# Routing half of the tokens of the first expert phase inside the recurrence, and the other half beside the expert tiles

## What is computed

```
logits = h @ router_w.T                      # 2048 x 8 experts
probs = softmax(logits)
vals, idx = top_k(probs, 2)
vals = vals / vals.sum(axis=-1)
# for each expert: y = (silu(gate) * up) @ dp.T, weighted by its vals and summed
```

## Time and profile before

| | us |
|---|---|
| median of 3 runs | 1005.97 |
| lowest and highest | 1000.86, 1021.48 |
| the profiled execution, its time | 1002.44 |
| the profiled execution, its span | 1000.6 |
| PE, DVE, ACT, POOL busy | 714.5, 504.5, 290.2, 286.6 |

### The profile page before, as it was taken

One profiled execution on the slowest core, in us unless ns is written; L12 is line 12 of the kernel. 1 busy time (PEld: TensorE's weight loads), 2 busy tenths in 40 slices (PEclk: granted clock), 3 DMA queues, 4 the chain that ended last, 5 costly groups with the idle time before them and its releaser, 6 DMA issues. The chain is left out here.

```text
span 1000.6 us, 13964 instructions
## 1 busy us (share of the span) xinstructions
PE 714.5 (71%) x4667; PEld 551.6 (55%) x4667; DVE 504.5 (50%) x1074; ACT 290.2 (29%) x561; POOL 286.6 (29%) x360
## 2 busy tenths in 40 slices
PE   2078898964524999971246999999999750999980
PEld 1056676743522776650135777787777550677660
DVE  5828697796270223545535455645564244222433
ACT  1014323231001444430102334433444300444430
POOL 2300111201037103417610233423343407402305
PEclk9997798885655999995555778977987955999995
DMA  9700000000123334422155442244220033434534
GB/s 318 253 1 0 1 1 1 1 0 0 43 85 127 121 101 141 130 76 81 37 65 64 65 65 34 41 57 65 33 34 2 1 80 120 143 101 122 174 122 126
DMA packets 63225, 75.78 MB, mean 76 GB/s; under 512 B 9410, under 2 KB 57930, under 8 KB 62550
## 3 DMA queue, kind: packets, MB, share of 16 engines
q1 hardware_dynamic: 57014, 58.11, 24.4%
q0 software_dynamic: 6144, 16.79, 5.3%
HBM read 33.56 MB, written 28.57 MB: 62 GB/s over the span
## 5 line engine op out<-in xcount | busy, mean ns | idle before, releaser
L974 PE MATMUL bank<-f_wgu,f_xt 128*128 x368 | 131.5, 481 | 6.5 <-ACT f_xt L1032 3.3
L1136 DVE TENSOR_TENSOR f_hid<-f_act_g,bank 128x176 f32<-128x176 f32 x92 | 31.1, 338 | 177.9 <-ACT f_act_g L1039 177.9
L911 POOL DMA_INDIRECT f_back<-ys,f_slots x64 | 63.0, 984 | 171.6 <-DMA ys<-f_yout 140.2
L997 PE MATMUL bank<-f_wd,f_hT 88*128 x368 | 95.2, 381 | 0.0
L974 PEld LDWEIGHTS bank<-f_wgu,f_xt 128*128 128x128 f32 x368 | 67.2, 195 | 40.9 <-issue 16.3
L900 POOL DMA_INDIRECT xs<-xn,f_slots x64 | 62.9, 983 | 68.3 <-DVE f_lv L1122 27.4
L1431 POOL TENSOR_SCALAR_AFFINE_SELECT b_prob<-b_prob 128x512 f32<-128x512 f32 x60 | 38.2, 637 | 150.7 <-ACT b_prob L1721 150.7
L1721 ACT ACTIVATE b_prob<-bank 128x1024 f32<-128x1024 f32 x60 | 61.5, 1025 | 58.6 <-PE bank L1553 58.3
L997 PEld LDWEIGHTS bank<-f_wd,f_hT 88*128 88x128 f32 x368 | 62.9, 190 | 5.7
L959 PE MATMUL bank<-ident_sb,f_xin 128*128 128x128 f32 x184 | 37.2, 286 | 38.9 <-DMA f_xin<-xs 38.4
L1795 DVE COPY_PREDICATED bank<-b_later,bank 128x512 f32<-128x512 int32 x60 | 41.4, 690 | 38.8 <-PE bank L1524 36.9
(11 more groups left out here) (294 smaller groups left out, 1659.4 us busy)
## 6 DMA issues: line engine op xcount, KB each, us to landing
f_xin<-xs SPq DMA_DIRECT2D x92, 128.0 KB, 2.2
ys<-f_yout SPq DMA_DIRECT2D x92, 128.0 KB, 1.7
xs<-f_zero SPq DMA_DIRECT2D x2, 2944.0 KB, 21.6
b_QS<-b_qh SPq DMA_DIRECT2D x32, 128.0 KB, 4.4
b_KS<-b_kh SPq DMA_DIRECT2D x32, 128.0 KB, 4.9
f_wd<-in_wd SPq DMA_DIRECT2D x4, 968.0 KB
f_wgu<-in_wgu SPq DMA_DIRECT2D x2, 1408.0 KB, 8.6
x_tok<-in_x SPq DMA_DIRECT2D x4, 512.0 KB, 5.6
```

The source lines that it names most:

```text
L911: pool.indirect_dma_start(back[:, n % GB, e], None, ys[h], bass.IndirectOffsetOnAxis(slots[:, h, e, i:i + 1], 0)).then_inc(got[n % GB], 16)
L974: mm = pe.matmul(psG[:, g % 2, 0:2 * FH], xt[:, g % 2, k * P:(k + 1) * P], w["gu"][:, k, bass.ds(e, 2 * FH)], start=k == 0, stop=k == KD - 1)
L997: mm = pe.matmul(psY[:, g % 2, 0:D], hT[:, g % 2, k * P:(k + 1) * P], wd[:, k, bass.ds(e, D)], start=k == 0, stop=k == 1)
```

## The change

The expert phase's state and semaphores move into one object, `Routed`, that lives through the whole program (`m` in the diff), and the routing chain is cut into named pieces of the class `Routing`.

- In the first phase, half 0 is routed in the recurrence. Iteration 2 has its logits (32 matmuls after `value_or_gate(3, 3)`) and its pieces `take`, `compare_equal`, `compare`, `choose`, `take_counts` on DVE; iteration 3 has `experts`, `slots`, `difference` behind `mean_squares`. PE waits for `TAKEN` ahead of `project_out` and for `COPIED` ahead of `betas`, since the PSUM banks are shared. POOL issues 12 of the 16 scatters between the last chunk's `rms` and its `tail_pool`, and 4 behind it.
- In the first phase itself only the logits of half 1 stand ahead of the tiles. The rest of its routing is spread over steps 1 to 9, its scatters come when `slots` is done in step 5, its exponential in step 8.
- In the second phase (`HOIST[1]` is False) half 0 is routed ahead of the tiles as before, and half 1 beside them. `ranks` of half 0 now stands ahead of the logits of half 1.
- The ranks are copied from PSUM to SBUF, one more operation per half. In the first phase SP issues the `wd` DMAs behind the loads of tiles 0 and 1. Logits and ranks go to another PSUM bank. The norm of the combined tokens is written to `xn`.
- The same pieces run in the same order within a half, except that `both` is made ahead of `pick`. `at` is None and `SPREAD_COMBINE` False, so code under them does nothing here.

```diff
+        ROUTED_AT = NCH // 2
+        SENT_AHEAD = 12
...
+                    if it == ROUTED_AT:
+                        pe.wait_ge(tl.xl_ready, now(it - 1))
+                        pe_logits(pe, m, xTh, xTl, 0, psY[:, 0])
                     rms_spread(it)
...
                         value_or_gate(it + 1, VT + 1)
+                    if it == ROUTED_AT:
+                        pe.wait_ge(m.route, routed(0, 0, TAKEN))
                     project_out(it)
+                    if it == ROUTED_AT:
+                        pe_ranks(pe, m, 0, 0, psB[:, 0])
+                        pe.wait_ge(m.route, routed(0, 0, COPIED))
                     if ahead:
                         betas(it + 1)
...
+                pairs = [(i, c) for i in range(NTH) for c in range(2)]
                 for it in range(0, NCH):
                     pool.wait_ge(ms_ready, now(it))
                     pool.wait_ge(rT_ready, before(it))
                     pool.tensor_tensor(rms[:], ms[:], minus_half[:, 0:TPC * HA], ALU.pow).then_inc(rms_ready, 1)
+                    if it == NCH - 1:
+                        for i, c in pairs[:SENT_AHEAD]:
+                            pool_scatter(pool, m, xn, 0, 0, i, c)
                     tail_pool(pool, tl, it)
+                for i, c in pairs[SENT_AHEAD:]:
+                    pool_scatter(pool, m, xn, 0, 0, i, c)
...
+                first = Routing(dve, m, 0, 0)
                 for it in range(NCH):
                     ahead = it + 1 < NCH
                     if ahead:
                         start(it + 1)
                     mean_squares(it)
+                    if it == ROUTED_AT + 1:
+                        first.experts()
+                        first.slots()
+                        first.difference()
                     if ahead:
                         decays(it + 1)
                         taps(it + 1, 0)
                     rms_split(it)
                     if ahead:
                         taps(it + 1, 1)
+                    if it == ROUTED_AT:
+                        first.take(psY[:, 0])
                     outputs(it)
+                    if it == ROUTED_AT:
+                        first.compare_equal()
+                        first.compare()
+                        first.choose()
                     if ahead:
                         taps(it + 1, 2)
+                    if it == ROUTED_AT:
+                        first.take_counts(psB[:, 0])
+                    if ahead:
                         taps(it + 1, 3)
                     tail_stats_dve(dve, tl, it, add=True)
...
+RANKS_AT, SHARES_AT = 3, 8
...
+TAKEN, RANKED, COPIED, EXPERTS_KNOWN, SLOTS_KNOWN, DIFF_KNOWN, SHARED = 2, 10, 12, 19, 29, 32, 35
...
+def pe_ranks(pe, m, turn, h, dst):
+    pe.wait_ge(m.route, routed(turn, h, RANKED))
+    chosen = m.both[:].rearrange("p e i -> p (e i)")
+    pe.matmul(dst[:, 0:NE * NTH], m.tri[:], chosen, start=True, stop=True)
+    pe.matmul(dst[:, NE * NTH:2 * NE * NTH], m.ones[:], chosen, start=True, stop=True).then_inc(m.pre_ready, 1)
...
+    def choose(self):
+        dve, m = self.dve, self.m
+        by_expert = m.rank[:].rearrange("p t e -> p e t")
+        self.step(dve.tensor_reduce(m.rank[:], m.cmp1[:].rearrange("p t (e j) -> p t e j", e=NE), AX.X, ALU.add))
+        self.step(dve.tensor_scalar(m.both[:], by_expert, 1.5, None, ALU.is_lt))
+        self.step(dve.tensor_scalar(m.pick[:, 0], by_expert, 0.0, None, ALU.is_equal))
+        self.step(dve.tensor_scalar(m.pick[:, 1], by_expert, 1.0, None, ALU.is_equal))
+        assert self.n == RANKED
+
+    def take_counts(self, src):
+        dve, m = self.dve, self.m
+        dve.wait_ge(m.pre_ready, 2 * self.turn + self.h + 1)
+        self.step(dve.tensor_copy(m.pre[:], src[:, 0:NE * NTH]))
+        self.step(dve.tensor_copy(m.tot[:], src[:, NE * NTH:2 * NE * NTH]))
...
+    def shares(self):
+        dve, m, h = self.dve, self.m, self.h
+        mine = slice(h * NTH, (h + 1) * NTH)
+        self.n = DIFF_KNOWN
+        dve.wait_ge(m.ex_done, 2 * self.turn + h + 1)
+        self.step(dve.tensor_scalar(m.den[:], m.ratio[:, h], 1.0, None, ALU.add))
+        self.step(dve.reciprocal(m.share[:, 0, mine], m.den[:]))
+        self.step(dve.tensor_tensor(m.share[:, 1, mine], m.share[:, 0, mine], m.ratio[:, h], ALU.mult))
+        assert self.n == SHARED
+
+
+def act_ratio(act, m, turn, h):
+    act.wait_ge(m.route, routed(turn, h, DIFF_KNOWN))
+    act.activation(m.ratio[:, h], m.diff[:, h], ACT.Exp).then_inc(m.ex_done, 1)
+
+
+def pool_scatter(pool, m, xn, turn, h, i, c):
+    if i == 0 and c == 0:
+        pool.wait_ge(m.filled, 32)
+        pool.wait_ge(m.route, routed(turn, h, SLOTS_KNOWN))
+    pool.indirect_dma_start(m.xs[h], bass.IndirectOffsetOnAxis(m.slots[:, h, c, i:i + 1], 0), xn[:, h * NTH + i], None)\
+        .then_inc(m.sent[h], 16)
...
+                if not HOIST[turn]:
+                    for k in range(2):
+                        sp.dma_start(wd[:, k], m.wd_in_dram[k * FK:(k + 1) * FK]).then_inc(d_in, 16)
                 for s in range(-3, STEPS):
+                    if s == -1 and HOIST[turn]:
+                        for k in range(2):
+                            sp.dma_start(wd[:, k], m.wd_in_dram[k * FK:(k + 1) * FK]).then_inc(d_in, 16)
...
+                for h in range(1 - FIRST_HALF_HERE, 2):
                     for i in range(TH):
                         for c in range(2):
+                            pool_scatter(pool, m, xn, turn, h, i, c)
...
+                if FIRST_HALF_HERE:
+                    pe_logits(pe, m, xTh, xTl, 0, psZ)
+                    pe_ranks(pe, m, turn, 0, psZ[:, P:2 * P])
+                    pe.wait_ge(m.route, routed(turn, 0, COPIED))
+                pe_logits(pe, m, xTh, xTl, 1, psZ)
                 x_transposed(0)
                 for s in range(STEPS):
                     if s < G:
                         gate_up(s)
+                    if s == RANKS_AT:
+                        pe_ranks(pe, m, turn, 1, psZ[:, P:2 * P])
...
-                for h in range(2):
-                    act.wait_ge(route, routed(h, DIFF_KNOWN))
-                    act.activation(ratio[:], diff[:], ACT.Exp).then_inc(ex_done, 1)
+                act_ratio(act, m, turn, 0)
...
+                    if s == SHARES_AT:
+                        act_ratio(act, m, turn, 1)
...
+                first, second = Routing(dve, m, turn, 0), Routing(dve, m, turn, 1)
+                if FIRST_HALF_HERE:
+                    first.take(psZ)
+                    first.compare_equal()
+                    first.compare()
+                    first.choose()
+                    first.take_counts(psZ[:, P:2 * P])
+                    first.experts()
+                    first.slots()
+                    first.difference()
+                first.shares()
+                second.take(psZ)
                 for s in range(STEPS):
...
+                    if s == 1:
+                        second.compare_equal()
+                        second.compare()
+                    if s == 2:
+                        second.choose()
+                    if s == RANKS_AT + 1:
+                        second.take_counts(psZ[:, P:2 * P])
+                        second.experts()
+                    if s == RANKS_AT + 2:
+                        second.slots()
+                    if s == RANKS_AT + 3:
+                        second.difference()
+                    if s == SHARES_AT + 1:
+                        second.shares()
```

More of the change, by code:

```diff
@@ L61, in before, with build @@
     return it * n + k
-def build(nc, t, out, stop=4):
+def build(nc, t, out):
     ctx = ExitStack()
@@ L186, in _ @@
                 rec_load(sp)
-                wts_load(sp)
+                m.load(sp, t)
             @block.gpsimd
@@ L240, in build @@
         stored = sem("stored")
[L241 to L247, removed]
+        back = sb("back", [P, GB, 2, D])
+        common = (x, xn, xTh, xTl, stats, meanvar, vareps, rstd, minus_half, bank, sem)
+        experts(nc, m, back, *common, ffn_sems, ident, last=False)
+        attention(nc, t, m, *common, ident)
+        experts(nc, m, back, *common, ffn_sems, ident, last=True, out=out, stored=stored)
 def heads_of_tile(u):
@@ L770, in clear @@
[L770 to L784 removed]
+            sp.dma_start(self.xs[h].rearrange("(t p) d -> p t d", p=P),
+                         self.zero[:].unsqueeze(1).broadcast_to([P, SLOT_TILES, D])).then_inc(self.filled, 16)
@@ new lines, with routed, tile_no, unit_no @@
+HOIST = (True, False)
+SPREAD_COMBINE = False
+RANKS_AT, SHARES_AT = 3, 8
+WEIGHT_STEPS = (9, 10, 11, 12, 15)
+YB, GB = 3, 3
+NTH = T // P // 2
+NU = 2 * NTH
+NG = 2 * SLOT_TILES
+TAKEN, RANKED, COPIED, EXPERTS_KNOWN, SLOTS_KNOWN, DIFF_KNOWN, SHARED = 2, 10, 12, 19, 29, 32, 35
+def routed(turn, h, n):
+    return (2 * turn + h) * SHARED + n
+def tile_no(turn, j):
+    return turn * NG + j
+def unit_no(turn, c):
+    return turn * NU + c
+def uses(n, i, ring):
+    return (n - 1 - i) // ring + 1 if n > i else 0
```

(35 more changed lines are left out.)

448 lines of the change are left out of this document (209 added, 239 removed).

## The result

The changed kernel takes 972.32 us (median of 4 runs, 967.79 to 976.92). The ratio to the kernel before is 0.969, with a 95% interval of 0.9602 to 0.9778. Later, beside the experiments, it ran 17, 13 and 11 times more, with medians of 1004.51, 1004.0 and 1006.22. Against 1004 the forecast of 975.5 asks for 28.5 us; the changed kernel, repeated beside the last of these batches, was 27.6 faster (experiment 9).

A forecast was written before the change was run, and what follows sets the result against it. The head of the expert phases, where logits, routing and scatters precede the first tile, was taken as the bound. −37.0 + 5.4 + 0.7 + 0.2 + 1.3 + 0.5 + 1.7 + 0.3 = −26.9 gave 975.5 us, range 965 to 987.

The forecast's parts named there:

- Removed, 37.0: Head of the first phase: of 43.9 us before the first tile only half 1's logits, 6.9, stay; gain 37.0.
- DVE in iteration 2, 5.4, and PE's logits, 0.7: Recurrence, iteration 2: DVE's added routing pieces count in full, 5.4 us; added logits, some at low clock, cost 0.7.
- Iteration 3, 0.2, and the barrier, 0: Recurrence's end: 5.5 us of routing against a DVE pause of 5.35 costs 0.2; barrier waiting for scatter landing, 0, up to 2.
- POOL, 12 scatters end by 256.7, 2.1 in hand: Iteration 3: 12 scatters take 15.5 us, ending at 256.7 before `tail_pool` wants POOL at 258.83; they cost nothing.
- Load 2, 1.3 (bounds 0 to 3): First phase's start: load 2 queues behind 1.9 MB of `wd`, lands near 16 where PE wants it at 14.8; cost 1.3.
- DVE 0.5; ACT 1.7 in phase 1: Tile steps: half 1's routing on DVE costs 0.5 us per phase; table loads for step 8's exponential delay `gate_up` by 1.7.
- rival 1: PE's clock comes otherwise: rising sooner at the first tiles, 972; falling early in iteration 2, 979 to 980; chance 0.18.
- Second phase, net +0.3: Second expert phase: earlier `ranks` of half 0, less the extra copy, gain 1.9; DVE 0.5 and ACT 1.7 against it.
- Half 1's slack, 11: Tile steps: half 1's scatters have landed by phase time 56, load 23 is issued at about 67; 11 us in hand.
- Rival 2: Tile steps 6 to 14: scatters share DMA engines with tile loads; eight loads 0.8 late in both phases, 988; chance 0.07.
- Rival 4: Half 1's scatters stretch beside the tiles beyond 2.0 us each, making the kernel slower: 1036, or about 1011; chance 0.03.
- rival 3: First phase's start: barrier or SP sees half 0's last scatters 5 us late, `wd` holds load 2 for 3: 981; chance 0.10.

The follow-up runs named there:

- experiment 9: The changed kernel repeated unedited, on one chip beside two edited versions and the kernel before: 978.61 us, ratio 0.9719 to the kernel before.
- Experiment 1: Changed kernel without the part in the recurrence: half 0 routed at the start of both phases, half 1 beside the tiles; 1004.97 us, ratio 1.0011.
- experiment 8: Changed kernel with four more 128x512 DVE operations, result unused, behind `choose` in iteration 2; 976.86 us, ratio 0.9721.
- experiment 5: Changed kernel with all 16 scatters of half 0 behind `tail_pool`, none ahead of it; 992.97 us, ratio 0.9858.
- Experiment 6: Changed kernel with all 16 scatters of half 0 ahead of `tail_pool`, not 12; 981.28 us, ratio 0.9744.
- experiment 2: Changed kernel with the two `wd` DMAs issued in step 1, behind load 3 and not load 1; 966.08 us, ratio 0.9623.
- experiment 7: Changed kernel with half 1's ranks moved from step 3 to 12 and its exponential from 8 to 17; 992.88 us, ratio 0.9868.

## Why the prediction was right

The time (975.5 forecast, 972.3 and 978.6 measured) and the mechanism came out as predicted; sizes within the sum were off both ways. That the touched stages give -26.7 and -27.3 against -26.9 is in part luck: the misses by stage, up to 1.4 us, cancel, and the tiles of one kernel differ by 2 us between its two traces. By its own steps:

- **Removed, 37.0.** Measured 37.06. What carried it was to take the whole head from the earlier trace rows and leave 32 logits at the low clock in it, 6.9 forecast, 6.82 measured. Experiment 1 gives all of it back.
- **DVE in iteration 2, 5.4, and PE's logits, 0.7.** Together 6.1 forecast, 5.3 measured. The DVE term holds, and experiment 8 shows why it had to be counted in full. The 0.7 was too careful. I had a quarter of the logits at the low clock; in fact practically all of them ran at the high one (granted clock 0.98 in 197 to 200.9), one every 0.11 us against 0.21 in the head, where the clock is 0.50. It fell right behind them: the last value matmuls ahead of the logits come every 0.23 us, and those of the gates, from 203 on, every 0.43. The spread of `rms`, slow by then, ended at 203.0, just as DVE was through with `take`. The windows around both sets of logits:

```profile
196.00:204.00 8.00, 8.00 (x46) 6.68 (x45) 6.14 (x12) 5.71 (x7) 0.00 (x0) 0.80 0.00 0
270.00:278.00 8.00, 7.15 (x34) 7.13 (x34) 0.62 (x4) 1.49 (x2) 0.00 (x0) 0.50 0.64 151
```

- **Iteration 3, 0.2, and the barrier, 0.** Measured 0.9 and 0.65, the two largest misses by share. The routing in DVE's pause did cost 0.12 (`ms` to the cast of `rms` took 5.65, before 5.53). A further 0.44 came from neighbours of the scatters, which I had left out. Two DVE operations took longer than in the kernel before, whose rows are

```profile
246.89 0.96 DVE L700 CAST oh<-sq 128x1536 fp32r<-128x1536 f32 x1
...
255.66 1.22 DVE L130 TENSOR_TENSOR x_tok<-bank,x_tok 128x1024 f32<-128x1024 f32 x1 [6.03 <-PE bank L508]
...
260.28 1.38 DVE L143 TENSOR_SCALAR xn<-x_tok,meanvar,rstd 128x256 f32<-128x256 f32 x4 [1.53 <-issue]
```

 against 1.18 and 1.60 after, +0.22 each. The last 0.35 isn't the scatters': DVE's wait for PE's output projection grew from 6.03 to 6.38, and without scatters beside it (experiment 5) it was 6.65. The projection's matmuls come every 0.21 us at the low clock and every 0.12 at the high one, and the step between the two came 3.2 us after the first of them in the kernel before, 3.8 in the changed one. For the barrier I took 0 and gave 2 as the bound; the value chosen was wrong and the bound right. Experiment 5 shows that it waits for POOL; what it adds with four scatters left, 0.65, is the step that I had put at nothing.
- **POOL, 12 scatters end by 256.7, 2.1 in hand.** 258.5, with 2.4 in hand, as the iteration began 1.3 later and `vareps` came 0.7 later in it. Experiment 6 shows that what goes beyond is late: four more scatters take 5.1, and the iteration grew by 2.5.
- **Load 2, 1.3 (bounds 0 to 3); DVE 0.5; ACT 1.7 in phase 1.** Together 3.5 forecast, 2.4 measured, with terms that are wrong both ways. Load 2 cost PE 3.22, above the bound, though in the median of the seven traces with this order it was 1.35 (experiment 2). I had worked out the end of `wd` from a DMA share of 0.55 and a landing 1 us behind it. Load 2 was in fact used at phase time 16.7, not 16, and PE was ready for it at 13.4, not at 14.8, since the clock came back sooner: it was 0.94 in 282 to 287.5, where before PE stayed low for 12.4 us after the first tile. That is the half of rival 1 that speaks for the change, and in this trace it paid for much of load 2. ACT measured 1.49. DVE's 0.5 isn't seen at all: no wait for it between steps 2 and 7.
- **Second phase, net +0.3.** Measured +1.1: the head gave 2.0 (forecast 1.9), the tile steps took 3.1 (forecast 2.2), of which 1.2 is ACT's wait in the step after the exponential (forecast 1.7), and 1.0 a wait that the forecast didn't have, PE's `ranks` of half 1 queued ahead of tile work while DVE was not done with `pick`:

```profile
823.32 0.20 PE L876 MATMUL bank<-f_both,f_tri 128*128 128x64 bf16 x1 [1.01 <-DVE f_pick L920]
```

- **Half 1's slack, 11.** Load 23 was issued 15.7 behind the last scatter's landing, so more was in hand than forecast.
- **The rivals.** Rival 2 (loads beside scatters) fell: not one wait for a load between 287.51 and 331.26. In the other traces with half 1 beside the tiles single waits for a load stand beside the scatters, at most 1.1 us, far from eight at 0.8 each. Rival 4 (scatters stretch beside tiles) fell too: 1.27 us each, and with experiment 7 one sees what it would have cost. Of rival 3 the barrier and load 2 came true, at 0.65 and 3.2 where it had 5 and 3. (By its own terms it is 982, since 5 and 1.7 come on top of 975.5, and the bounds named with rival 1 reach down to 969, not 966; neither changes a chance.)

On the rule of the Trainium skill that I weighed (SBUF — State Buffer, the shared port pair): two of the twelve scatters in iteration 3, those beside the end of DVE's cast and its subtraction of 128x1536 elements, took 1.28 and 1.49 us instead of 0.96, and the cast 0.22 longer, which experiment 5 takes away. That agrees with the rule in kind. In size it doesn't: the page has 3100 ns for such a DMA, and no scatter here came near that. Beside the tiles' DVE operations there is no effect; in the kernel before, some scatters beside the comparisons of 128x512 took 1.14 to 1.27.

## What to carry to other kernels

A chain of small operations and DMA issues that stands in front of a pipeline can be worth its whole length, if its input is ready earlier; its price is then paid where the busiest engine of the earlier stage takes it in, to the full, and the pause of that engine takes the rest for nothing. Look at each queue that the moved work shares: here one edit put 1.9 MB ahead of a load that PE wanted next, and the end of a block waits until GpSimd has issued its last DMA, and some 2 us more. When two traces are compared, cut them into stages first, since untouched stages of this program differ by 4 us and more from one execution to the next.

## What the runs showed of the hardware

- A barrier at the end of a block waits until GpSimd has issued its indirect DMAs, and some 2 us more: 18.1 us from the last DVE operation to the first matmul with 16 scatters left, and that matmul 3.54 and 3.55 us after the last issue ended, in two kernels, against 1.94 and 1.44 behind the last DVE operation where no scatter was outstanding (the kernel before, experiment 6).
- The slowing beside a cast is mutual, as the lines above have it: scatters 0.96 to 1.28 and 1.49 us, a 128x1536 cast 0.96 to 1.18 and back to 0.96 in experiment 5, four 128x256 `xn` operations 1.38 to 1.60 and back to 1.38 in experiment 6. In experiment 6 the same two scatters, the sixth and seventh, took 1.28 and 1.50.
- Two loads of 128 KB issued ahead of 1.9 MB of weights landed after 2.1 us, the two issued right behind the weights after 15 us. SP's issuing took the usual 0.4 us each (its timeline; then its DMAs in 271.1 to 271.5 and in 272.4 to 273.2):

```profile
270.80 0.81 SPq L1115 DMA_DIRECT2D f_xin<-xs  x2
271.66 0.77 SPq L1128 DMA_DIRECT2D f_wd<-in_wd  x2
272.47 0.82 SPq L1115 DMA_DIRECT2D f_xin<-xs  x2
DMA to landing us min/median/max: 2.1/2.1/2.1
DMA to landing us min/median/max: 14.9/14.9/15.0
```
